# Audio tower on one Trainium2 core: when the first experts' tiles, their pads and their weights are requested

## The reference

```
h = layernorm(patches(x) @ W.T + b) * gamma + beta       # 128 sequences, 124 tokens each, 256 wide
h = h + attention(ln(h))                                 # one head, 124 keys
logits = relu(ln(h) @ rw1 + rb1) @ rw2 + rb2             # 6 experts
top two experts of each token, their weights w1, w2 from a softmax of the softmax's values
h = h + sum over the two: w * ((relu(relu(ln(h) @ W1 + b1) @ W2 + b2)) @ W3 + b3)
```

## Time and profile before

| | us |
|---|---|
| median of 3 runs | 1405.89 (1405.25 to 1407.78) |
| the profiled execution, time | 1404.13 |
| its span in the trace | 1402.3 |
| TensorE busy, all of the span | 1250.8 |
| VectorE, ScalarE, GpSimd busy | 1057.7, 841.6, 925.9 |
| mean granted clock | 0.953 |

### The profile page before, as it was taken

One profiled execution on the slowest core, in us unless ns is written; L12 is line 12 of the kernel. 1 busy time (PEld: TensorE's weight loads), 2 busy tenths in 40 slices (PEclk: granted clock), 3 DMA queues, 4 the chain that ended last, 5 costly groups with the idle time before them and its releaser, 6 DMA issues.

```text
span 1402.3 us, 26155 instructions
## 1 busy us (share of the span) xinstructions
PE 1250.8 (89%) x7888; PEld 1088.5 (78%) x7888; DVE 1057.7 (75%) x3581; ACT 841.6 (60%) x1838; POOL 925.9 (66%) x738
## 2 busy tenths in 40 slices
PE   4898999999999999999609899999999999999993
PEld 3787787888888788877407788888888888888882
DVE  3587888888888888887526577877878777777782
ACT  2376667666666667656305566666666666666661
POOL 1126777777777777777751476766677666766775
PEclk7899999999999999999758999999999999999996
DMA  3023444444444444445566698777967779789764
GB/s 113 27 60 96 105 118 111 116 116 107 111 120 114 107 114 119 115 103 158 165 191 225 178 227 195 123 119 136 290 112 123 119 159 252 127 181 239 120 86 49
DMA packets 141746, 190.95 MB, mean 136 GB/s; under 512 B 37795, under 2 KB 101670, under 8 KB 141606
## 3 DMA queue, kind: packets, MB, share of 16 engines
q0 software_dynamic: 75456, 69.19, 30.9%
q1 hardware_dynamic: 64886, 119.30, 26.9%
q10 hardware_dynamic: 1264, 0.79, 0.2%
HBM read 168.72 MB, written 98.79 MB: 191 GB/s over the span
## 4 chain that ended last, share of the span: by engine, by line
PE 45%; DVE 19%; POOL 15%; issue 7%; DMA 2%; SPq 2%; ACT 1%; POOLq 0%; DVEq 0%; ACTq 0%
PE bank L668 26%; PE bank L690 13%; POOL rstd L416 7%; POOL expert_rows L424 6%; PE bank L658 4%; DVE h L1018 3%; DVE h L981 3%; DVE y L975 3%; DVE xn1T_lo L944 2%; POOL out L474 2%; DVE stats L889 1%; POOL vareps L413 1%; DVE mxi L1056 1%; DVE negmax L938 1%; DMA out<-h 1%
## 5 line engine op out<-in xcount | busy, mean ns | idle before, releaser
L474 POOL DMA_INDIRECT out<-yo,tail x268 | 436.2, 1627 | 236.3 <-issue 148.3
L424 POOL DMA_INDIRECT expert_rows<-rec,row_i x256 | 348.4, 1361 | 77.1 <-issue 63.6
L847 ACT ACTIVATE h2v<-bank,small 128x512 f32<-128x512 f32 x134 | 92.4, 689 | 207.1 <-PE bank L668 207.1
L690 PE MATMUL bank<-w_sb,h_hi 128*128 128x256 f32 x1072 | 210.3, 290 | 2.0 <-DVE h_lo L1140 2.0
L668 PE MATMUL bank<-x_hi,w_sb 128*128 128x512 f32 x536 | 180.3, 398 | 13.8 <-issue 11.3
L668 PE MATMUL bank<-h_hi,w_sb 128*128 128x512 f32 x536 | 177.2, 391 | 0.9 <-DVE h_lo L1140 0.9
L690 PEld LDWEIGHTS bank<-w_sb,h_hi 128*128 128x128 f32 x1072 | 172.6, 193 | 2.8 <-DVE h_lo L1140 2.6
L690 PE MATMUL bank<-w_sb,h_lo 128*128 128x256 f32 x536 | 152.3, 284 | 0.0
L808 ACT ACTIVATE xn<-h,nmr,rstd 124x256 f32<-124x256 f32 x128 | 66.5, 590 | 121.4 <-DVE nmr L1010 121.4
L668 PEld LDWEIGHTS bank<-x_hi,w_sb 128*128 128x128 f32 x536 | 102.6, 191 | 39.1 <-issue 17.9
L853 ACT ACTIVATE yo<-yo,gcol 128x256 f32<-128x256 f32 x268 | 113.9, 498 | 16.9 <-DVE yo L1177 16.9
(11 more groups left out here) (176 smaller groups left out, 3169.7 us busy)
## 6 DMA issues: line engine op xcount, KB each, us to landing
w_sb<-split_weights SPq DMA_DIRECT2D x69, 1536.0 KB, 8.4
xg<-expert_rows SPq DMA_DIRECT2D x67, 530.0 KB, 4.5
out<-h SPq DMA_DIRECT2D x32, 496.0 KB
small<-in_esmall SPq DMA_DIRECT2D x69, 134.0 KB, 10.8
split_weights<-half_w SPq DMA_DIRECT2D x36, 256.0 KB, 3.0
x_in<-in_x SPq DMA_DIRECT2D x32, 250.0 KB, 12.8
raw_w<-in_eweights SPq DMA_DIRECT2D x36, 128.0 KB, 11.5
out<-yo,tail POOLq DMA_INDIRECT x268, 4.1
```

Source lines behind the costliest of these rows:

```text
L424: pool.indirect_dma_start(rows_dram, bass.IndirectOffsetOnAxis(ap=row_i[0:TOK, slot, j, k:k + 1], axis=0), rec[0:TOK, slot, j, :], None).t ...
L474: pool.indirect_dma_start(out, bass.IndirectOffsetOnAxis(ap=tail[:, s, j, E8:].bitcast(I32), axis=0), yo[:, ys, j, :], None, compute_op=AL ...
L690: mm = pe.matmul(banks[6 + b][:, (j % 2) * D:(j % 2 + 1) * D], act[:, c, j * P:(j + 1) * P], w[:, 2, c, wh, :], start=(c == 0 and p == 0), ...
L847: act.activation(h2v[:, m, :], banks[4 + m][:], ACT.Relu, bias=small[:, slot, DC + m:DC + m + 1]).then_inc(S["h2_v"], 1)
```

## The change

- **Pads on ACT's queue.** The six blocks are written by `write_pads`, called by ACT after its last group. POOL's very last indirect store waits for them (`pads_written`), so that one count covers both.
- **First four tiles' rows by a table of counts.** At group 28 DVE keeps the running counts of the experts (`t_seen`, `t_more`). Groups 29 to 31 all count on one semaphore, `scattered[1]`. From the counts and the tiles' rows DVE makes `need_tab` for tiles 0 to 3: `FIRST_SENT` if the tile's 512 rows are full with the first 29 groups, else `ALL_SENT`. SP waits for the groups up to 28, then for tile 0 to 3 each for that number (`first_tile_rows`), and stands in order: rows 0, rows 1, `small` and weights of tile 0, rows 2, `small` and weights of tile 1, rows 3.
- **Two weight slots, fetched by layer.** `w_sb` has two slots instead of four; a tile's weights are three transfers of 512 KB, each with its own semaphore and each requested when that layer of the tile two before is done (`load_layers`). `wload_tab` says whether the expert differs from that of the tile two before. `small` keeps four slots, with semaphores of its own. PE waits for each layer's weights.
- **Five areas of spare rows.** `expert_rows` ends in five areas of 512 rows, `out` in two. Alternate areas carry token numbers of the first and the second area of `out`, written from `pad_rows` and from slot 0 of `xg`, which POOL fills at the start. SP stores the seven blocks in iteration 5 instead of two at the start. The tiles that aren't needed read one area each, and only the first of them waits for the tile before.

```
+SPARE = NT - NTOK * TOPK // TILE
+LAST = 3
+LAST_SLOT = (G - LAST) % SENT
+FIRST_SENT = 16 * GB * TOPK * len(range(LAST_SLOT, G - LAST, SENT))
+ALL_SENT = FIRST_SENT + 16 * GB * TOPK * LAST
+ROWS_AT, NEEDS_AT, EXPERTS_AT, ADDS_AT = 12, 17, 19, 20
...
+        def write_pads(eng, experts):
+            eng.wait_ge(S["table"], 1)
+            for e in experts:
+                at = eng.value_load(pad_at[0:1, e:e + 1], min_val=0, max_val=NE * REGION)
+                eng.dma_start(rows_dram[bass.ds(at, TILE), :].rearrange("(p j) n -> p (j n)", p=P),
+                              pad_rows[:].rearrange("p j n -> p (j n)")).then_inc(S["pads_written"], 16)
...
+            def spare_rows():
+                for i in range(2):
+                    sp.dma_start(out[NTOK + i * TILE:NTOK + (i + 1) * TILE, :].rearrange("(p j) n -> p j n", p=P),
+                                 pad_rows[:, :, 0:D]).then_inc(S["dummy_cleared"], 16)
+                for i in range(SPARE):
+                    at = NE * REGION + i * TILE
+                    src = pad_rows[:] if i % 2 == 0 else xg[:, 0, :, :]
+                    sp.dma_start(rows_dram[at:at + TILE, :].rearrange("(p j) n -> p (j n)", p=P),
+                                 src.rearrange("p j n -> p (j n)")).then_inc(S["dummy_cleared"], 16)
+            sp.wait_ge(S["pool_const"], 18)
             def step(it, group_of):
+                if it == DEPTH:
+                    spare_rows()
...
+            def load_layers(t, layers):
+                expert = expert_of(t)
+                fresh = sp.value_load(wload_tab[0:1, bass.ds(t, 1)], min_val=0, max_val=1)
+                for n in layers:
+                    sp.dma_start(w_sb[t % WSLOTS][:, n, :, :, :].rearrange("p c b n -> p c (b n)").bitcast(F32),
+                                 split_dram[bass.ds(expert * (3 * DC) + n * DC, DC), :, :].rearrange("q p n -> p q n"),
+                                 cond=fresh != 0).then_inc(w_loaded[t % WSLOTS][n], 16)
...
+            def first_tile_rows(t):
+                row = row_of(t)
+                sp.wait_ge(S["table"], NEEDS_AT)
+                need = sp.value_load(need_tab[0:1, t:t + 1], min_val=FIRST_SENT, max_val=ALL_SENT)
+                wait_apart(sp, scattered[LAST_SLOT], need, S["sp_passed"])
+                load_rows(t, row)
+            for i in range(SENT):
+                sp.wait_ge(scattered[i], 16 * GB * TOPK * len(range(i, G - LAST, SENT)))
+            sp.wait_ge(S["dummy_cleared"], 16 * (2 + SPARE))
+            sp.wait_ge(S["table"], ROWS_AT)
+            first_tile_rows(0)
+            first_tile_rows(1)
+            sp.wait_ge(S["table"], EXPERTS_AT)
             sp.wait_ge(S["first_loaded"], 32 * AHEAD)
...
+            load_small(0)
+            load_layers(0, range(3))
+            first_tile_rows(2)
+            load_small(1)
+            load_layers(1, range(3))
+            first_tile_rows(3)
+            load_small(2)
+            load_small(3)
+            sp.wait_ge(scattered[LAST_SLOT], ALL_SENT)
...
+            next_rows(SLOTS)
+            for t in range(NT):
+                if t + WSLOTS < NT:
+                    wait_apart(sp, S["h1_ps"], (t + 1) * 2, S["sp_passed"])
+                    load_layers(t + WSLOTS, (0,))
+                next_rows(t + SLOTS + 1)
+                if 1 <= t < NT - 1:
+                    wait_apart(sp, S["y_ps"], t * 2, S["sp_passed"])
+                    load_layers(t + 1, (2,))
+                if 1 <= t < NT - SLOTS + 1:
+                    wait_apart(sp, S["y_dve"], t * 4, S["sp_passed"])
+                    load_small(t + SLOTS - 1)
+                if t + WSLOTS < NT:
+                    wait_apart(sp, S["h2_ps"], (t + 1) * 2, S["sp_passed"])
+                    load_layers(t + WSLOTS, (1,))
...
             def scatter(g, pieces):
                 slot = g % SENT
+                sent = scattered[slot if g < G - LAST else LAST_SLOT]
                 for n in pieces:
+                    if g == G - 1 and n == GB * TOPK - 1:
+                        pool.wait_ge(S["pads_written"], 16 * NE)
...
+                if x4 and x4[0] == G - LAST - 1:
+                    seen = place[0:1, x4[1], GB, :]
+                    v.wait_ge(S["pos"], x4[0] * POS_N + 1)
+                    v.tensor_copy(t_seen[:], seen)
+                    v.tensor_tensor(t_more[:, 0:NE - 1], seen[:, 1:NE], seen[:, 0:NE - 1], ALU.subtract
+                                    ).then_inc(S["seen"], 1)
...
-            made(v.tensor_scalar(row_tab[:], t_row[:], float(NE * REGION), None, ALU.min))
+            made(v.tensor_copy(row_tab[:], t_row[:]))
...
-            v.tensor_tensor(t_new[:, 1:NT], t_new[:, 1:NT], t_ge[:, 1:NT, NE - 1], ALU.max).then_inc(S["dve_const"], 1)
```

More of the change, by code:

```diff
@@ L202, in audio_tower @@
         rows_loaded = [sem(f"rows_loaded{i}") for i in range(SLOTS)]
-        w_loaded = [sem(f"w_loaded{i}") for i in range(SLOTS)]
+        w_loaded = [[sem(f"w{n + 1}_loaded{i}") for n in range(3)] for i in range(WSLOTS)]
+        small_loaded = [sem(f"small_loaded{i}") for i in range(SLOTS)]
         y_added = [sem(f"y_added{i}") for i in range(2)]
@@ L237, in bank_read, with fetched @@
                     return
+        def fetched(slot, rnd):
+            return (rnd * (SLOTS // WSLOTS) + slot // WSLOTS + 1) * 16
         def landed(t, slot, rnd):
@@ L313, in _ @@
             pipeline(step)
[L316 to L323, removed]
@@ L325, in expert_of @@
-            def expert_of(t):
[L326 to L336, removed]
+            def expert_of(t):
+                return sp.value_load(exp_tab[0:1, bass.ds(t, 1)], min_val=0, max_val=NE - 1)
@@ L338, in row_of, with load_small @@
+            def load_small(t):
+                expert = expert_of(t)
+                fresh = sp.value_load(load_tab[0:1, bass.ds(t, 1)], min_val=0, max_val=1)
+                sp.dma_start(small[:, t % SLOTS, :], esmall[bass.ds(expert, 1), :, :].rearrange("o p n -> (o p) n"),
+                             cond=fresh != 0).then_inc(small_loaded[t % SLOTS], 16)
             def row_of(t):
-                return sp.value_load(row_tab[0:1, bass.ds(t, 1)], min_val=0, max_val=NE * REGION)
+                return sp.value_load(row_tab[0:1, bass.ds(t, 1)], min_val=0, max_val=NE * REGION + (SPARE - 1) * TILE)
@@ L353, in _ @@
[L353 to L372, removed]
@@ L374, in _, with next_rows @@
-            tiles(load_tile)
+                sp.wait_ge(w_stored[i], 16 * (NCHUNK // RING))
+            load_small(0)
[7 more added lines that the diff above has]
+            sp.wait_ge(scattered[LAST_SLOT], ALL_SENT)
+            def next_rows(t):
+                if t < NT:
+                    wait_apart(sp, S["txT_ps"], (t - SLOTS + 1) * 2, S["sp_passed"])
+                    wait_apart(sp, S["tail_kept"], (t - SLOTS + 1) * 2, S["sp_passed"])
+                    load_rows(t % SLOTS, row_of(t))
@@ L455, in _ @@
             pipeline(step)
-            pool.wait_ge(S["routed"], 1)
-            pool.wait_ge(S["table"], 15)
+            for i in range(RING):
+                pool.wait_ge(h2_stored[i], 16 * uses(i, RING))
+            pool.wait_ge(S["dummy_cleared"], 16 * (2 + SPARE))
+            pool.wait_ge(S["table"], ADDS_AT)
             def add_tile(t, slot, rnd):
@@ L819, in _ @@
             pipeline(step)
+            write_pads(act, range(NE))
             def read_rows(t):
@@ L1219 @@
         args.append(nc.dram_tensor(f"in_{name}", v.shape, mybir.dt.from_np(v.dtype), kind="ExternalInput").ap())
-    out = nc.dram_tensor("out", [NTOK + TILE, D], F32, kind="ExternalOutput").ap()
+    out = nc.dram_tensor("out", [NTOK + 2 * TILE, D], F32, kind="ExternalOutput").ap()
     audio_tower(nc, *args, out)
```

63 lines of the change are left out of this document (38 added, 25 removed).

## The result

The changed kernel takes 1381.62 us (median of 4 runs, 1380.74 to 1381.95), the kernel before 1405.57 on the same chip: a ratio of 0.9831, 95% interval 0.9808 to 0.9854, so 24 us less. The profiled executions have spans of 1402.3 before and 1378.9 after, 23.4 us apart; that is what the traces have to account for.

A forecast was written before the change was run, and what follows sets the result against it. TensorE bounds it, apart from the gap, tile-part stalls and tail. Terms 0.9 + 0.3 + 0 - 14.3 - 7.4 - 4.5 - 4.9 = -29.9 took 1404.13 to 1374.2, 1376 as median; range 1369 to 1389.

The forecast's parts named there:

- the likeliest case: Whole kernel: all terms come as summed, 1376 us, its own range 1371 to 1382; chance 0.60.
- Start, +0.9: Kernel start: POOL's extra clear and iota delay ACT's first table load, +0.9 us on the chain (bounds 0.3 and 1.5).
- Spare rows, "Cost 0; bound +3": Iteration 5: seven stores ahead of group 6's x_in, 14 us at most, 11 us of cover; cost 0, bound +3.
- Counts and gap, -14.3: Between groups and tiles: early rows start tile 0 sooner, tile 1 waits for the last scatter; -14.3 us (bounds -17 and -10).
- Early stalls, -7.4: Tiles 1 to 8: fewer weight fetches shorten add landings, stalls 3.5 instead of 10.9 us; -7.4 (bounds -10.9 and 0).
- Later stalls, -4.5: Later changes of expert: weight thirds delay landings too little to stall, 0.5 instead of 5.0 us; -4.5 (bounds -5 and 0).
- tail, -4.9: Last tiles: only tile 64 still waits for its predecessor, tile 66's adds at 1386.0, not 1390.86; -4.9 us (bounds -5.5, -2).
- no wait on TensorE: Tile part: each third of weights is asked for about 15 us before use, against landings of 4 to 10.
- Shared engines: Gap: early rows and pads share the DMA engines, delaying the last scatter to 738 and tile 1: 1381 us; chance 0.12.
- Adds set the pace: Tile part: add landings stay at 8.5 us despite fewer fetches, so both stall gains vanish: 1388 us; chance 0.12.
- SP's queue the bound: Tile part: SP's nine register loads and five transfers per tile make the kernel slower, about 1408 us; chance 0.04.
- Early request fails: Gap: tile 0 is held to the last scatter too, so nothing is gained there: 1390 us; chance 0.02.

The follow-up runs named there:

- the kernel with SP's pads: Changed kernel with stores spread, last scatter not awaiting pads and tile 1's flags first, plus pads written by SP instead of ACT: 1372.27 us, ratio 0.9771.
- the flags: Changed kernel with tile 1's small and weight flags ahead of tile 2's rows in SP's queue: 1382.32 us, ratio 0.9869.
- the scatter without pads: Changed kernel with POOL's last scatter not waiting for the pads; SP waits for them before tile 2's rows: 1381.9 us, ratio 0.9863.
- the held pads: Changed kernel with stores spread, last scatter not awaiting pads, tile 1's flags first, and ACT's pads after SP's requests for rows 0 and 1: 1371.98 us, ratio 0.9777.

## Why the prediction came out as it did

1381.62 lies in the range of 1369 to 1389, and at the upper end of the likeliest case's own (1371 to 1382). It is 5.6 above the 1376, and the parts say where from. That it lies in the likeliest case's range is partly luck: the gap's term came near by another path than the one reasoned.

**Start, +0.9: not settled.** In the changed kernel's trace nothing of it is left at group 3, but in the eleven experiments 0.3 to 1.6 us are there at group 5, which fits the 0.9. What of it reaches the counts can't be read under the spread of the groups' part.

**Spare rows, "Cost 0; bound +3": wrong, and the largest miss: the part up to the counts was put at +1.2 and measured +5.2.** The step put the cost at nothing, although its own 14 us of issuing are 3 more than its 11 us of cover. The stores' issue stands ahead of the load's own landing: `x_in` left SP 15.8 us later, and then took 14.5 us to land where the earlier trace rows has a median of 12.8. In the terms known beforehand, 108.39 + 14 + 12.8 = 135.2 against 132.22 makes +3; the rest of the 6.6 at group 6 is the pace of the stores, 15.9 us instead of 14, and the landing, 14.5 instead of 12.8. Their 10 us of data are not a third term: the landing behind them grew by 1.7 us only. The experiment with spread stores shows that the cost goes with their place. It is about 7 us at group 29; that only 5.2 show at the counts is within what the last groups vary by.

**Counts and gap, -14.3: -11.7, and the reason was another.** "So tile 1, and with it everything later, waits for the last scatter" doesn't hold. Tile 1 started on TensorE 10.5 us behind tile 0, and the wait for its flags, behind the last scatter, was 0.25 us of that. So tile 0's own path set it, and the scatter's ended only just behind. That path was mis-sized: rows 0 requested 8.9 us behind the counts (7.3 put; `need_tab` was there at +5.6 as put, but SP then took 3.2 us instead of 1.7), 11.9 us to transposes (8.5 put), L1(0) 4.6 later as put. The landing is the larger error: the "8.0 us, the pads' median" was taken for rows that go out beside the pads, where they took 11.9, and without these they land in 3.4 to 4.6 us. The last scatter left at 735.56 and had landed by 740.68, not at 733. It did tile 1 little harm, 0.25 us here and 1.16 with the stores spread, and the rest little, since moving its issue and the flags changed no time beyond the noise.

So three paths end nearly together, read from the counts: tile 0's rows and TensorE's work on two tiles (L1(1) at +35.8); the flags of tile 1's weights behind SP's request of tile 2 (it comes at +32.4); and tile 2's rows by the same request (in the kernel with SP's pads L1(2) came 12.2 us behind its request, which by estimate makes +44.6 here, where TensorE itself came to tile 2 at +45.2). To shorten one gives nothing, as the flags, the scatter without pads, the held pads and the pads on SP's queue have each shown. What might shorten all three, less data in the stretch, wasn't tried.

**Early stalls, -7.4: -6.4.** The steps between the adds of tiles 0 to 3 are 11.1, 12.5 and 11.5, where one of 13 and then 10.4 were put, so "I take one step of 13, then 10.4" erred by the later ones; they sum to 35.0 against 33.8. That the fixed wait for a landing makes the stalls is shown by its removal (0.3 us left). That the landings are longer by the traffic of weights is shown in part: with the fetches put back the steps sum to 40.2, but of its 10.3 us of stalls some 4 are another wait and the clock behind it. And 2.1 of the 10.9 us before were the clock, not a wait. The kernels with the changed kernel's fetches and waits vary from 4.0 to 6.7 in this part, so its size is known to about 2 us.

**Later stalls, -4.5: -4.8, and tail, -4.9: -5.6: right in mechanism and nearly in size.** Putting back each cause brings back its time: 7.7 us of stalls, and 36.6 us of tail. But "no wait on TensorE" for a third of the weights isn't quite so: behind the 0.25 us of tile 1 it sat 0.17 us at 763.15 and 0.52 us at 779.84, 0.7 us in all. In the tail tile 65 follows 7.7 behind tile 64 (7.9 put), and tile 66 only 7.4 further, since its values were ready.

**The rivals.** *Shared engines* is right in its cause and its time (1381), wrong in its place: the pads slow the rows, yet it is the rows of tile 0 that pay, not tile 1 by way of the scatters. The last scatter did land "after 738", which the prediction named as a sign of being wrong, and it did not decide. The gap makes 2.6 us of the 6.5 by which the sum was off; the part ahead of the counts makes 4.0. *Adds set the pace*: refuted, stalls went from 15.9 to 4.7. *SP's queue the bound*: refuted by 597 of 600 us busy; SP's loads of `exp_tab` by line (min/median/max ns) do reach long values, but not in each tile:

```profile
L350 SPq TENSOR_LOAD <-exp_tab x264: 3/270/2475, 722.5 to 1345.5; - x132
```

*Early request fails*: refuted, it is worth 13.6 us by the experiment. Left open is why `pad_at` varies by 4 us between kernels whose groups' part is the same (705.3 to 709.3), and 6 us between those that spread the stores. Open is also why the latter reach `pad_at` 0.5 to 6.4 us sooner than the kernel before (703.16), though at group 29 the kernel with the stores spread alone is only 0.3 us ahead.

## What to carry to other kernels

The time to issue a bunch of stores comes on top of the full landing time of whatever stands behind them in one queue: put long stores behind the loads of an iteration and one per iteration, not in a bunch ahead of them. A landing time read from one stretch belongs to the traffic of that stretch; before a transfer's median is used elsewhere, ask what will be on the engines beside it. When paths of equal length meet, undo or shorten each alone first: here four changes to the gap gave nothing that the times show. And a wait that leaves TensorE idle for several us can cost more than its length, since the clock may be lower behind it: look at the granted clock of the tile after.

## What the hardware showed that was not expected

A 0.5 MB store holds the issuing queue for 1.5 to 3.0 us when others are ahead of it (2.34 and 2.31 for the first two of seven, 2.96 and 3.00 for two later ones), while a request with few bytes ahead of it takes 0.34. ACT's requests block its own activations in the same way: six pads held it for 10.6 to 13.6 us, and the evacuation behind them waited (25.01 us of idle time, ended by issue). From the last scatter's issue to the request that waits for it 11.2 us passed with 3 MB of pads and 1 MB of rows on the way, and 5 once they had landed; loads of 0.5 MB rows took 3.4 us on empty engines, 11.9 beside the pads. Behind 6.05 us of idle TensorE the granted clock was 0.85 over the next tile, behind waits of 1.45 us it stayed at 1.00.
